# A norm's last multiply as an item of its own, and the routing in eight pieces, among the scan units on VectorE

## The chip, the cores and the metric

The kernel runs on one core of one Trainium2 chip. The metric is the device time of one execution in microseconds (us); less is better. The engines are called TensorE (PE, with PEld for its weight loads), VectorE (DVE), ScalarE (ACT), GpSimd (POOL) and SyncE (SP, which here only issues DMAs).

## What is computed

The input is x of 8 batches x 256 positions x 256 features. Each batch passes three blocks in turn:

```
x = x + 0.5 * ffn(layernorm(x))      # f1
x = x + mamba_block(layernorm(x))    # mixer, then MLP
x = x + 0.5 * ffn(layernorm(x))      # f2, the same weights as f1

ffn(x):     scores = sigmoid(x @ gate_w)           # 32 experts
            top 6 of the scores, divided by their sum -> combine
            sum over experts of combine * (silu(x@wg) * (x@wu)) @ wd,  plus a shared expert
block(x):   h = x + mixer(rmsnorm(x));  h + mlp(rmsnorm(h))
mixer(h):   projections z, x, B, C, dt;  conv of 4 taps;  dt = softplus(...)
            h_t = exp(dt*A) * h_(t-1) + dt*x*B     # 512 channels x 16 states, over 256 positions
            y = sum over states of h_t * C;  y * silu(z) @ out_proj
```

Every expert is computed for every position (26 chunks of 128 hidden features: 24 routed, 2 shared), and the combine weights zero most of them.

## The kernel before, in words

Data lie with features on partitions and positions along the free dimension. The program is a list of **items** for each step t (`items_of`, from L129), and every engine walks the same list and does its own part of each item (`walk`). The steps overlap the batches: in step t batch t is in f1 (`first`), batch t-1 in the mixer (`mamba`), batch t-2 in the MLP (`mlp`) and batch t-3 in f2 (`second`). Steps t=3 to t=6 have everything in them and are four turns of a hardware loop; the others are written out, from t=-1 (load, norm and routing of the first batch) to t=10.

**The heavy list** is the MLP's chunks (`gum`, `down`) and the feed-forward's chunks. Chunk p is made of `g` (6 matmuls in three passes over split halves, L595 to L597), ScalarE's tanh (L824), `by_g` (VectorE, L957), `u` (6 matmuls), `by_u` (VectorE, L963), `by_comb` (GpSimd multiplies by the combine weights, L1218) and `down` (L675). f1 and f2 share the chunks: their positions lie side by side, 512 columns. There are three PSUM banks for `g` and `u` (`gub`) and three for everything small (`side`); an engine that wants a bank waits until the use three before it has been read.

**The light list** is norms and projections (`along`), then 32 scan **units** with the norms and routings among them, then `yz`, `outp` and the norm rms2. A unit is one pair of states of 128 channels: `ub` is a matmul that spreads B (L765) and VectorE's product (L1103), on ScalarE two exponentials (L921); `unit` is VectorE's scan (L1112), a matmul that spreads C (L768), VectorE's product (L1118) and GpSimd's add to a sum (L1228, L1231). After the eighth unit of a group GpSimd adds the halves and the sum to y (L1234, L1238). `yz` (L1122) gates y when the last sum is there.

**A norm** is `n1` and `n2`. For ln1, lnA and ln2 `n1` is a mean on TensorE (L690), VectorE's subtraction (L1001) and ScalarE's square (L834); for rms1 and rms2 only the square. `n2` is the mean of the squares on TensorE (L698), ScalarE's Ln and Exp with -0.5 into the one `rstd` tile (L837, L840, each with its table load), and VectorE's multiply by rstd: L1015 for ln1, ln2 and lnA, two of L1011 for rms1 and rms2. **A routing** `rt1` is 8 small matmuls (L711), ScalarE's exp (L843), and on VectorE `route` (L1131): 19 instructions that count up the semaphore `routing`, most of them waiting for the one before them. `rt2` in the next step uses its result.

**The order** comes from `merge` (L176): two lists are laid over each other by the share of their summed lengths (`LENGTH` where f1 and f2 are both there, else `SHORT`). First the units and the two norm-and-routing chains are merged (ln2's chain in the first half of them, ln1's in the second), and the result, behind `along`, is merged with the heavy list. On VectorE and GpSimd `late_order` then sets an item back by up to `LAG` items, but not past the next light item. `GROWS` tells by how much each item raises each semaphore, and `USES` who frees a `side` bank; the waits are worked out from them.

Of the kernel before, what the change touches and what calls it, by code (L numbers as in the profile page):

```python
# [35 lines left out]
KC = DM // P  # L36
EXPERTS, FEXP, TOPK, FSH = 32, 96, 6, 192
# [8 lines left out]
TT = SEQ // P  # L46
# [9 lines left out]

GROWS = {
# [50 lines left out]
def kind_of(item):  # L108
# [3 lines left out]
    if item[0] == "n2":  # L112
        return "n2r" if item[1] in ("rms1", "rms2") else "n2c"
# [14 lines left out]

def items_of(t):  # L129
# [4 lines left out]
    if t < 0:  # L134
        return [("load",), ("n1", "ln1"), ("n2", "ln1"), ("rt1", "f1")]
# [4 lines left out]
    norms = [("n1", "lnA"), ("n2", "lnA"), ("n1", "rms1"), ("n2", "rms1")] if mamba else []  # L140
# [15 lines left out]
    if not mamba:  # L156
# [11 lines left out]
SHORT = {"n1": 3, "n2": 8.0, "split": 2.25, "x": 5, "z": 3,  # L168
          "dt": 3, "sp": 3, "sp_dt": 3, "sp_x": 2, "y0": 2,
          "ub": 2, "unit": 2, ("unit", UNITS - 1): 8, "rt1": 8,  # L170
# [39 lines left out]
def ffn_items(t, first, second):  # L210
# [8 lines left out]
    for p in range(FFN_CHUNKS + DLAG):  # L219
# [20 lines left out]
LAG = {"n1": 0, "n2": 3, "split": 0, "x": 0, "z": 1, "dt": 0, "sp": 1, "sp_dt": 0,  # L240
       "sp_x": 0, "y0": 0, "ub": 0, "unit": 1, "rt1": 3, "outp": 4,
# [9 lines left out]
def late_order(items):  # L251

    out, held, left = [], None, 0
    for it in items:
# [6 lines left out]
        else:  # L261
# [7 lines left out]
    "side": {"n1c": [("centered", 1)], "n2c": [("logged", 1)],  # L269
             "n2r": [("logged", 1)], "rt1": [("rt_exp", 1)], "rt2": [("comb_ready", 1)],  # L270
# [47 lines left out]
def macaron_kernel(nc, d):  # L318
# [13 lines left out]
    with ctx:  # L332
# [249 lines left out]
        def _(pe):  # L582
# [18 lines left out]
            def do(s, it):  # L601
# [99 lines left out]
                elif kind == "rt1":  # L701
# [3 lines left out]
                    pe.wait_ge(sem["normed"], s.count("normed", ("n2", norm), 1))  # L705
# [20 lines left out]
                elif kind in ("z", "x", "split"):  # L726
                    if kind == "split" and it[1] == 0:
                        pe.wait_ge(sem["normed"], s.count("normed", ("n2", "rms1"), KC))
# [57 lines left out]
        def _(act):  # L786
# [5 lines left out]
            def do(s, it):  # L792
# [33 lines left out]
                elif kind == "n1":  # L826
# [3 lines left out]
                    elif it[1] == "rms1":  # L830
                        act.wait_ge(sem["normed"], s.count("normed", ("n2", "lnA"), 1))
                    else:
                        act.wait_ge(sem["mixed"], s.count("mixed", ("outp",), 1))
# [94 lines left out]
        def _(dve):  # L928
# [13 lines left out]
            def do(s, it):  # L942
# [48 lines left out]
                elif kind == "r0":  # L991

                    dve.wait_ge(sem["normed"], s.count("normed", ("n2", "lnA"), 1))
# [9 lines left out]
                elif kind == "n2":  # L1003
                    dve.wait_ge(sem["rstd"], s.count("rstd", it, 1))
# [11 lines left out]
                elif kind == "rt1":  # L1016
# [114 lines left out]
            def route(s, it):  # L1131


                done = [0]
# [14 lines left out]
                for tt in range(TT):  # L1149
                    link(v.max(top8[:, tt, :], sc[:, tt, 0:EXPERTS]))  # L1150
                settle()
                link(v.tensor_copy(top8[:, :, TOPK:8], marks[:]))
                settle()
                link(v.memset(pace[:], 0.0))
                for tt in range(TT):
                    link(v.match_replace(rep[:, tt, :], top8[:, tt, :], sc[:, tt, :], 0.0))
                settle()
                link(v.tensor_tensor(cm[:], sc[:, :, 0:EXPERTS], rep[:, :, 0:EXPERTS], ALU.subtract))
                settle()
                link(v.tensor_reduce(csum[:], cm[:], axis=AX.X, op=ALU.add))  # L1160
                settle()
                link(v.tensor_scalar(csum[:], csum[:], 1e-20, None, ALU.add))
                settle()
                link(v.reciprocal(csum[:], csum[:]))
                settle()
                for tt in range(TT):
                    link(v.tensor_scalar(cm[:, tt, :], cm[:, tt, :], csum[:, tt:tt + 1], None, ALU.mult))
                settle()
                E = EXPERTS
                out = c3[it[1]]  # L1170
                link(v.tensor_copy(out[:, :, 0:E], cm[:]))
                settle()
                link(v.tensor_tensor(cm[:], cm[:], out[:, :, 0:E], ALU.subtract))
                settle()
                link(v.tensor_copy(out[:, :, E:2 * E], cm[:]))
                settle()
                link(v.tensor_tensor(out[:, :, 2 * E:3 * E], cm[:], out[:, :, E:2 * E], ALU.subtract))
                assert done[0] == 19
# [139 lines left out]
```

## Time and profile before

| | us |
|---|---|
| median of 3 executions | 1938.59 (1936.56 to 1942.36) |
| the profiled execution, its time | 1936.02 |
| its span, first to last instruction | 1934.2 |
| mean granted TensorE clock in it | 0.934 of full speed |

Times within the profile count from the start of the span. The rows of the section below are of this one execution. In them a line number is one of the kernel before; "busy" is the time in which an engine had an instruction, and the idle time before an instruction stands in brackets with what ended it. PEclk is the clock that TensorE was granted, as a share of 2.4 GHz.

### The profile page before, as it was taken

To read this page: it belongs to the slowest core of one execution; us is meant where nothing else is said; L and a number is where in the kernel's file an instruction comes from. 1 tells how busy PE (TensorE), PEld (TensorE's weight loads), DVE (VectorE), ACT (ScalarE), POOL (GpSimd) and SP (SyncE) were. 2 spreads that over 40 slices of the span, in tenths; PEclk is the share of its full clock that TensorE was granted. 3 is DMA by queue.
4 is the path that set the end of the run, shared out by engine and by line. 5 is a ranking of instruction groups with operands and counts; after the bars stand their busy time and mean duration, and the time that the engine had idled before them with its cause. 6 is when DMAs were issued, how large, how long until landed. Compare 5 with 4: busy or idle time off the path is not lost. (4 is left out here: it accounts for less than half of the span.)

```text
span 1934.2 us, 25234 instructions
## 1 busy us (share of the span) xinstructions
PE 1601.1 (83%) x7512; PEld 1194.2 (62%) x7512; DVE 1295.1 (67%) x2331; ACT 705.1 (36%) x1418; POOL 720.2 (37%) x838
## 2 busy tenths in 40 slices
PE   6776768677978988789888989788988998678999
PEld 5665557555755557455664557555675567556888
DVE  3236984688468964789466974689648974896343
ACT  4234424433352425333343423433244334432211
POOL 4411552244134532345223542245324542353222
PEclk9887889878999999899998999899999999988999
DMA  7752223323232222222231223222232223323563
GB/s 260 281 170 91 86 86 99 111 88 98 78 106 72 81 89 74 105 74 80 80 104 65 84 77 95 85 77 88 81 98 93 87 77 86 126 88 101 174 205 133
DMA packets 72751, 204.77 MB, mean 106 GB/s; under 512 B 12928, under 2 KB 22368, under 8 KB 72224
## 3 DMA queue, kind: packets, MB, share of 16 engines
q1 hardware_dynamic: 64416, 177.86, 27.7%
q0 software_dynamic: 8192, 25.17, 4.5%
q8 instruction: 69, 1.13, 0.2%
q14 instruction: 74, 0.61, 0.1%
HBM read 179.39 MB, written 15.73 MB: 101 GB/s over the span
## 5 line engine op out<-in xcount | busy, mean ns | idle before, releaser
L595 PE MATMUL gub<-x_hi,wr 128*128 128x256 f32 (+1 forms) x1144 | 460.5, 403 | 83.5 <-DVE hid L963 60.6
L675 PE MATMUL acc<-hid,w_down 128*128 128x256 f32 (+1 forms) x1144 | 423.9, 498 | 0.9 <-DVE hid L963 0.8
L1218 POOL TENSOR_TENSOR hid<-hid,weight 128x256 f32<-128x256 f32 (+1 forms) x264 | 263.5, 998 | 428.0 <-DVE hid L963 409.9
L824 ACT ACTIVATE hid<-gub 128x256 f32<-128x256 f32 (+1 forms) x350 | 160.9, 460 | 680.5 <-PE gub L597 590.5
L596 PE MATMUL gub<-x_lo,wr 128*128 128x256 f32 (+1 forms) x1144 | 395.7, 346 | 0.0
L597 PE MATMUL gub<-x_hi,wr 128*128 128x256 f32 (+1 forms) x1144 | 394.7, 345 | 0.0
L1231 POOL TENSOR_TENSOR ring<-ring 128x512 f32<-128x512 f32 x192 | 245.8, 1280 | 314.4 <-DVE ring L1118 314.4
L1112 DVE TENSOR_TENSOR_SCAN ring<-decays,side 128x512 f32<-128x512 f32 x256 | 310.7, 1214 | 4.1 <-DVE side L1103 1.5
L595 PEld LDWEIGHTS gub<-x_hi,wr 128*128 128x128 f32 x1144 | 231.9, 203 | 122.1 <-issue 73.9
L675 PEld LDWEIGHTS acc<-hid,w_down 128*128 128x128 f32 x1144 | 212.9, 201 | 88.3 <-issue 68.8
L596 PEld LDWEIGHTS gub<-x_lo,wr 128*128 128x128 f32 x1144 | 232.3, 203 | 21.1 <-issue 4.3
L597 PEld LDWEIGHTS gub<-x_hi,wr 128*128 128x128 f32 x1144 | 230.5, 201 | 23.5
L921 ACT ACTIVATE decays<-dts,a_neg 128x255 f32<-128x255 f32 x512 | 223.5, 497 | 50.8 <-DVE ring L1112 40.8
L957 DVE SCALAR_TENSOR_TENSOR hid<-hid,gub 128x256 f32<-128x256 f32 (+1 forms) x286 | 153.7, 537 | 97.0 <-ACT hid L824 97.0
L1103 DVE TENSOR_TENSOR side<-dtx,side 128x512 f32<-128x512 f32 x256 | 176.8, 690 | 31.2 <-PE side L765 30.7
L1118 DVE TENSOR_TENSOR ring<-ring,side 128x512 f32<-128x512 f32 x256 | 176.0, 688 | 32.1 <-PE side L768 6.5
L963 DVE TENSOR_TENSOR hid<-hid,gub 128x256 f32<-128x256 f32 (+1 forms) x286 | 153.7, 537 | 52.1 <-PE gub L597 49.8
L768 PE MATMUL side<-cst,sel_c 96*128 96x256 bf16 x512 | 108.1, 296 | 80.6 <-DVE ring L1112 76.0
L765 PE MATMUL side<-bst,sel_b 96*128 96x256 bf16 x512 | 108.8, 297 | 50.4 <-DVE ring L1112 40.6
L1197 POOL TENSOR_TENSOR pool_pace<-eps_col 128x1 f32<-128x1 f32 x128 | 29.6, 231 | 297.5 <-PE gub L637 183.0
L768 PEld LDWEIGHTS side<-cst,sel_c 96*128 96x128 bf16 x512 | 37.3, 103 | 148.9 <-DVE ring L1112 102.9
L739 PE MATMUL side<-dts,w_in 128*128 128x256 f32 x448 | 110.3, 395 | 21.4 <-DVE z L1028 12.6
(115 smaller groups left out, 1725.4 us busy)
## 6 DMA issues: line engine op xcount, KB each, us to landing
wr<-w_halves SPq DMA_DIRECT2D x260, 512.0 KB, 3.3
wm_gu<-in_w_mlp POOLq DMA_DIRECT2D x64, 256.0 KB, 3.0
w_halves<-wr SPq DMA_DIRECT2D x26, 512.0 KB, 4.9
wm_down<-in_w_mlp POOLq DMA_DIRECT2D x64, 128.0 KB, 2.6
w_raw<-in_w_gu SPq DMA_DIRECT2D x26, 256.0 KB, 4.7
cst<-decays SPq DMA_DIRECT2D x192, 32.0 KB, 1.9
xin<-in_x SPq DMA_DIRECT2D x8, 256.0 KB, 3.4
x<-in_x SPq DMA_DIRECT2D x8, 256.0 KB, 2.6
```

The source lines that it names most:

```text
L595: mm(out, w[:, 0, half, k, :], x_hi[:, k, a:b], start=(k == 0), stop=False)
L596: mm(out, w[:, 0, half, k, :], x_lo[:, k, a:b], start=False, stop=False)
L597: last = mm(out, w[:, 1, half, k, :], x_hi[:, k, a:b], start=False, stop=(k == KC - 1))
L675: last = mm(acc[k][:, a:b], w, h[:, a:b], start=(c == 0), stop=(c == (MLP_CHUNKS if mlp else FFN_CHUNKS) - 1))
L824: A(hid[c % HSLOTS][:, a:b], s.gub_of(it)[:, a:b], ACT.Tanh, scale=0.5).then_inc(sem["tanh_done"], 1)
L921: A(decay[u % 2][:, h, 1:SEQ], dts[:, j, 1:SEQ], ACT.Exp, scale=a_neg[:, j, n:n + 1]).then_inc(sem["decay"], 1)
L957: v.scalar_tensor_tensor(h, h, 1.0, s.gub_of(of)[:, a:b], ALU.add, ALU.mult).then_inc(sem["gated"], 1)
L1103: v.tensor_tensor(b, twice(dtx[:, j, :]), b, ALU.mult).then_inc(sem["driven"], 1)
L1112: v.tensor_tensor_scan(w.rearrange("p h s -> p (h s)"), decay[u % 2][:, :, :].rearrange("p h s -> p (h s)"), s.side_of(("ub", u))[:, :], 0 ...
L1118: v.tensor_tensor(w, w, pair(s.side_of(it)), ALU.mult).then_inc(sem["read_out"], 1)
L1218: nc.gpsimd.tensor_tensor(h, h, weight[c // 3 % CSLOTS][:, a:b], ALU.mult).then_inc(sem["weighted"], 1)
L1231: add(ysum, ysum, ring[:, u % 3], ALU.add).then_inc(sem["y_sum"], 1)
```

## The change

`n2` ends with rstd on ScalarE; VectorE's multiply is the new item `nm`, placed behind it by the length of `n2` (3, or 6 in `SHORT`). `rt1` ends with ScalarE's exp; VectorE's 19 instructions become eight items `rq` of 2, 3, 1, 3, 2, 2, 2 and 4 instructions, each of length 0.75. The order within a routing and the instructions are as before; each piece but the first begins with a wait for the piece before it. `LAG` is 3 for `nm` and 0 for `n2`, `rt1` and `rq`, so on VectorE a routing is no longer set back. Those who waited for `n2`'s product now wait for `nm`'s. Cut to its core:

```diff
+ROUTE = (2, 3, 1, 3, 2, 2, 2, 4)
...
-    "n2c": {"side_filled": 1, "logged": 1, "rstd": 1, "normed": 1},
-    "n2r": {"side_filled": 1, "logged": 1, "rstd": 1, "normed": KC},
-    "rt1": {"side_filled": 1, "rt_exp": 1, "routing": 19},
+    "n2": {"side_filled": 1, "logged": 1, "rstd": 1},
+    "nmc": {"normed": 1},
+    "nmr": {"normed": KC},
+    "rt1": {"side_filled": 1, "rt_exp": 1},
+    **{f"rq{i}": {"routing": links} for i, links in enumerate(ROUTE)},
...
+def norm(which):
+    return [("n1", which), ("n2", which), ("nm", which)]
+
+
+def routing(call):
+    return [("rt1", call)] + [("rq", call, i) for i in range(len(ROUTE))]
...
-    norms = [("n1", "lnA"), ("n2", "lnA"), ("n1", "rms1"), ("n2", "rms1")] if mamba else []
+    norms = norm("lnA") + norm("rms1") if mamba else []
...
-    last = [("yz",), ("outp",), ("n1", "rms2"), ("n2", "rms2")] if mamba else []
+    last = [("yz",), ("outp",)] + norm("rms2") if mamba else []
...
-    ln2 = [("n1", "ln2"), ("n2", "ln2"), ("rt1", "f2")] if mlp else []
-    ln1 = [("n1", "ln1"), ("n2", "ln1"), ("rt1", "f1")] if following else []
+    ln2 = norm("ln2") + routing("f2") if mlp else []
+    ln1 = norm("ln1") + routing("f1") if following else []
...
-LENGTH = {"n1": 3, "n2": 5, "split": 2.25, "x": 10.0, "z": 3,
+LENGTH = {"n1": 3, "n2": 3, "nm": 2, "rq": 0.75, "split": 2.25, "x": 10.0, "z": 3,
...
-          "ub": 2, "unit": 2, ("unit", UNITS - 1): 8, "rt1": 8,
+          "ub": 2, "unit": 2, ("unit", UNITS - 1): 8, "rt1": 2,
...
-SHORT = {"n1": 3, "n2": 8.0, "split": 2.25, "x": 5, "z": 3,
+SHORT = {"n1": 3, "n2": 6.0, "nm": 2.0, "rq": 0.75, "split": 2.25, "x": 5, "z": 3,
...
-LAG = {"n1": 0, "n2": 3, "split": 0, "x": 0, "z": 1, "dt": 0, "sp": 1, "sp_dt": 0,
-       "sp_x": 0, "y0": 0, "ub": 0, "unit": 1, "rt1": 3, "outp": 4,
+LAG = {"n1": 0, "n2": 0, "nm": 3, "rq": 0, "split": 0, "x": 0, "z": 1, "dt": 0, "sp": 1, "sp_dt": 0,
+       "sp_x": 0, "y0": 0, "ub": 0, "unit": 1, "rt1": 0, "outp": 4,
...
-                elif kind == "n2":
-                    dve.wait_ge(sem["rstd"], s.count("rstd", it, 1))
+                elif kind == "nm":
+                    dve.wait_ge(sem["rstd"], s.count("rstd", ("n2", it[1]), 1))
...
-                dve.wait_ge(sem["rt_exp"], s.count("rt_exp", it, 1))
-                link(v.tensor_scalar(e_sc[:], e_sc[:], 1.0, None, ALU.add))
-                settle()
-                link(v.reciprocal(sc[:, :, 0:EXPERTS], e_sc[:]))
-                settle()
-                link(v.memset(pace[:], 0.0))
...
+                if piece == 0:
+                    dve.wait_ge(sem["rt_exp"], s.count("rt_exp", ("rt1", it[1]), 1))
+                    link(v.tensor_scalar(e_sc[:], e_sc[:], 1.0, None, ALU.add))
+                    settle()
+                    link(v.reciprocal(sc[:, :, 0:E], e_sc[:]))
+                else:
+                    settle()
+                if piece == 1:
+                    link(v.memset(pace[:], 0.0))
+                    for tt in range(TT):
+                        link(v.max(top8[:, tt, :], sc[:, tt, 0:E]))
+                elif piece == 2:
+                    link(v.tensor_copy(top8[:, :, TOPK:8], marks[:]))
+                elif piece == 3:
+                    link(v.memset(pace[:], 0.0))
+                    for tt in range(TT):
+                        link(v.match_replace(rep[:, tt, :], top8[:, tt, :], sc[:, tt, :], 0.0))
+                elif piece == 4:
+                    link(v.tensor_tensor(cm[:], sc[:, :, 0:E], rep[:, :, 0:E], ALU.subtract))
+                    settle()
+                    link(v.tensor_reduce(csum[:], cm[:], axis=AX.X, op=ALU.add))
+                elif piece == 5:
+                    link(v.tensor_scalar(csum[:], csum[:], 1e-20, None, ALU.add))
+                    settle()
+                    link(v.reciprocal(csum[:], csum[:]))
+                elif piece == 6:
+                    for tt in range(TT):
+                        link(v.tensor_scalar(cm[:, tt, :], cm[:, tt, :], csum[:, tt:tt + 1], None, ALU.mult))
+                elif piece == 7:
+                    link(v.tensor_copy(out[:, :, 0:E], cm[:]))
+                    settle()
+                    link(v.tensor_tensor(cm[:], cm[:], out[:, :, 0:E], ALU.subtract))
+                    settle()
+                    link(v.tensor_copy(out[:, :, E:2 * E], cm[:]))
+                    settle()
+                    link(v.tensor_tensor(out[:, :, 2 * E:3 * E], cm[:], out[:, :, E:2 * E], ALU.subtract))
+                assert done[0] == ROUTE[piece]
```

## Rows read from the trace of the kernel before

**Rows 1.** The page: span, and busy time with its share of the span.

```profile
span 1934.2 us, 25234 instructions
PE 1601.1 (83%) x7512; PEld 1194.2 (62%) x7512; DVE 1295.1 (67%) x2331; ACT 705.1 (36%) x1418; POOL 720.2 (37%) x838
```

**Rows 2.** Windows by step, t=3, t=5 and t=7: window, its length, then each engine.

```profile
core 0: us, PE busy (x) PEld busy (x) DVE busy (x) ACT busy (x) POOL busy (x), PEclk, DMA share, GB/s
498.00:717.00 219.00, 187.80 (x775) 126.84 (x773) 159.01 (x272) 84.07 (x161) 84.83 (x92) 0.98 0.26 83
942.00:1167.00 225.00, 194.09 (x780) 131.00 (x780) 158.87 (x271) 84.07 (x161) 85.02 (x92) 0.95 0.26 84
1392.00:1594.00 202.00, 184.41 (x766) 125.32 (x765) 153.38 (x250) 79.76 (x155) 83.80 (x92) 0.98 0.29 91
```

**Rows 3.** Windows of stages within t=5, among the scan units; same columns.

```profile
1012.50:1062.00 49.50, 39.94 (x151) 24.94 (x149) 34.74 (x62) 15.82 (x31) 18.30 (x16) 0.86 0.20 65
1034.00:1052.00 18.00, 16.67 (x75) 10.77 (x73) 15.00 (x33) 5.90 (x13) 10.27 (x9) 1.00 0.19 63
1062.00:1144.30 82.30, 75.05 (x323) 46.63 (x322) 76.20 (x117) 31.35 (x65) 44.06 (x37) 1.00 0.25 84
1028.40:1033.80 5.40, 5.40 (x15) 3.99 (x16) 2.50 (x4) 0.00 (x0) 1.28 (x1) 0.50 0.23 77
1055.80:1061.10 5.30, 5.30 (x12) 2.70 (x13) 1.56 (x3) 0.82 (x2) 0.17 (x1) 0.50 0.00 0
1122.30:1144.00 21.70, 19.07 (x84) 11.99 (x84) 20.86 (x28) 6.47 (x14) 11.62 (x10) 1.00 0.22 74
```

**Rows 4.** Timeline of t=5 at the norms ln2 and ln1: start, us, instruction, idle before.

```profile
1025.85 0.69 DVE L1015 TENSOR_TENSOR xc_f<-xc_f,rstd 128x512 f32<-128x512 f32 x1 [4.10 <-ACT rstd L840]
1028.33 0.61 PE L768 MATMUL side<-cst,sel_c 96*128 96x256 bf16 x2 [4.16 <-DVE ring L1112]
...
1099.39 0.69 DVE L1015 TENSOR_TENSOR xc_f<-xc_f,rstd 128x512 f32<-128x512 f32 x1 [2.38 <-ACT rstd L840]
```

**Rows 5.** Timeline of t=5 at f2's routing, its first and last instruction among them.

```profile
1048.05 0.20 DVE L1144 TENSOR_SCALAR e_sc<-e_sc 128x64 f32<-128x64 f32 x1 [0.94 <-ACT e_sc L843]
...
1049.19 1.03 DVE L1152 COPY top<-marks 128x4 f32<-128x4 f32 x1
...
1052.92 0.23 DVE L1177 TENSOR_TENSOR c_f<-cm,c_f 128x64 bf16<-128x64 f32 x1
...
1055.74 0.61 PE L768 MATMUL side<-cst,sel_c 96*128 96x256 bf16 x2 [3.42 <-DVE ring L1112]
```

**Rows 6.** Groups by line (busy us, mean ns, idle), then single lines (ns min/median/max).

```profile
L1231 POOL TENSOR_TENSOR ring<-ring 128x512 f32<-128x512 f32 x192 | 245.8, 1280 | 314.4 <-DVE ring L1118 314.4
L1112 DVE TENSOR_TENSOR_SCAN ring<-decays,side 128x512 f32<-128x512 f32 x256 | 310.7, 1214 | 4.1 <-DVE side L1103 1.5 <-ACT decays L921 0.8
L1144 DVE TENSOR_SCALAR e_sc<-e_sc 128x64 f32<-128x64 f32 x16 | 8.5, 532 | 7.9 <-ACT e_sc L843 7.9
L1152 DVE COPY top<-marks 128x4 f32<-128x4 f32 x16 | 7.5, 470 | 0.6
...
L1152 DVE COPY top<-marks x16: 169/171/1054, 16.2 to 1840.9; 128x4 f32<-128x4 f32 x16
L1158 DVE TENSOR_TENSOR cm<-sc,rep x16: 224/226/785, 17.4 to 1841.6; 128x64 f32<-128x64 f32 x16
```

**Rows 7.** Waits over the whole span: us in total, times, longest.

```profile
DVE xc_f L1015 <- ACT rstd L840: 50.6, 16, 5.1
DVE xs L1122 <- POOL xs L1238: 19.4, 8, 2.7
```

**Rows 8.** TensorE's first projection behind rms1 in t=5; VectorE's multiply of an MLP chunk.

```profile
962.58 3.72 PE L739 MATMUL side<-dts,w_in 128*128 128x256 f32 x16 [1.09 <-DVE dts L1011]
...
L949 DVE TENSOR_TENSOR hid<-hid,gub 128x256 f32<-128x256 f32 x64 | 26.9, 421 | 2.2
```

More of the change, by code:

```diff
@@ L111, in kind_of @@
         return "n1r" if item[1] in ("rms1", "rms2") else "n1c"
-    if item[0] == "n2":
-        return "n2r" if item[1] in ("rms1", "rms2") else "n2c"
+    if item[0] == "nm":
+        return "nmr" if item[1] in ("rms1", "rms2") else "nmc"
+    if item[0] == "rq":
+        return f"rq{item[2]}"
     if item[0] in ("wl", "wln"):
@@ L134, in items_of @@
     if t < 0:
-        return [("load",), ("n1", "ln1"), ("n2", "ln1"), ("rt1", "f1")]
+        return [("load",)] + norm("ln1") + routing("f1")
     hand = ([("hx", "f1")] if first else []) + ([("hx", "f2")] if second else [])
@@ L159, in items_of @@
     return hand + heavy[:6] + keep + merge(heavy[6:-TAIL], along + scan, length) + heavy[-TAIL:]
-LENGTH = {"n1": 3, "n2": 5, "split": 2.25, "x": 10.0, "z": 3,
+LENGTH = {"n1": 3, "n2": 3, "nm": 2, "rq": 0.75, "split": 2.25, "x": 10.0, "z": 3,
           "dt": 3, "sp": 3, "sp_dt": 3, "sp_x": 2, "y0": 2,
-          "ub": 2, "unit": 2, ("unit", UNITS - 1): 8, "rt1": 8,
+          "ub": 2, "unit": 2, ("unit", UNITS - 1): 8, "rt1": 2,
           "yz": 3.9, "outp": 3, "g": 1.3, "u": 1.3, "down": 1.7, "gum": 1.7, "cmb": 0.2}
-SHORT = {"n1": 3, "n2": 8.0, "split": 2.25, "x": 5, "z": 3,
+SHORT = {"n1": 3, "n2": 6.0, "nm": 2.0, "rq": 0.75, "split": 2.25, "x": 5, "z": 3,
           "dt": 3, "sp": 3, "sp_dt": 3, "sp_x": 2, "y0": 2,
-          "ub": 2, "unit": 2, ("unit", UNITS - 1): 8, "rt1": 8,
+          "ub": 2, "unit": 2, ("unit", UNITS - 1): 8, "rt1": 2,
           "yz": 3.9, "outp": 3, "g": 1.3, "u": 1.3, "down": 1.7, "gum": 1.7, "cmb": 0.2}
@@ L268 @@
 USES = {
-    "side": {"n1c": [("centered", 1)], "n2c": [("logged", 1)],
-             "n2r": [("logged", 1)], "rt1": [("rt_exp", 1)], "rt2": [("comb_ready", 1)],
+    "side": {"n1c": [("centered", 1)], "n2": [("logged", 1)],
+             "rt1": [("rt_exp", 1)], "rt2": [("comb_ready", 1)],
              "z": [("z_done", 1)], "x": [("x_padded", 1)],
@@ L704, in do @@
                     norm = "ln1" if it[1] == "f1" else "ln2"
-                    pe.wait_ge(sem["normed"], s.count("normed", ("n2", norm), 1))
+                    pe.wait_ge(sem["normed"], s.count("normed", ("nm", norm), 1))
                     for over, least in s.last_use("side", it):
@@ L727, in do @@
                     if kind == "split" and it[1] == 0:
-                        pe.wait_ge(sem["normed"], s.count("normed", ("n2", "rms1"), KC))
+                        pe.wait_ge(sem["normed"], s.count("normed", ("nm", "rms1"), KC))
                         if first_mamba[0]:
@@ L830, in do @@
                     elif it[1] == "rms1":
-                        act.wait_ge(sem["normed"], s.count("normed", ("n2", "lnA"), 1))
+                        act.wait_ge(sem["normed"], s.count("normed", ("nm", "lnA"), 1))
                     else:
@@ L991, in do @@
                 elif kind == "r0":
-                    dve.wait_ge(sem["normed"], s.count("normed", ("n2", "lnA"), 1))
+                    dve.wait_ge(sem["normed"], s.count("normed", ("nm", "lnA"), 1))
                     if ("end", "mlp") in s.at:
@@ L1015, in do @@
                         v.tensor_tensor(dst[:], dst[:], twice(rstd[:, :]), ALU.mult).then_inc(sem["normed"], 1)
-                elif kind == "rt1":
+                elif kind == "rq":
                     route(s, it)
@@ L1131, in route @@
             def route(s, it):
+                E = EXPERTS
+                out, piece = c3[it[1]], it[2]
                 done = [0]
@@ L1141, in settle @@
                     dve.wait_ge(sem["routing"], s.count("routing", it, done[0]))
-                dve.wait_ge(sem["rt_exp"], s.count("rt_exp", it, 1))
-                link(v.tensor_scalar(e_sc[:], e_sc[:], 1.0, None, ALU.add))
-                settle()
-                link(v.reciprocal(sc[:, :, 0:EXPERTS], e_sc[:]))
-                settle()
-                link(v.memset(pace[:], 0.0))
-                for tt in range(TT):
-                    link(v.max(top8[:, tt, :], sc[:, tt, 0:EXPERTS]))
@@ L1151, in route @@
[L1151 to L1178, printed above, removed]
+                if piece == 0:
[5 more added lines that the diff above has]
+                    settle()
```

## The prediction

> **What bounds the kernel now.** The page's busy times come first [rows 1]: TensorE is busy 83% of the span, VectorE 67%. Neither share says what a change on VectorE is worth, because the work differs by stage. The windows by step [rows 2] show that the steps with everything in them take 219 to 225 us, of which TensorE is busy 188 to 194 and VectorE 159. Step numbers are those of the planner; t=3 to t=6 are four turns of one loop. The stages of one such turn [rows 3] show more. From 1062 to 1144.3, among the scan units, VectorE is busy 76.20 of 82.30 us, and in a quiet piece of it 20.86 of 21.70, so 0.96 is what it reaches: VectorE sets the pace there. From 1012.5 to 1062 it is busy only 34.74 of 49.50 us, and TensorE 39.94, although the same mix of work stands there. So something is waited for.
>
> The chain of waits in order of time says what. At 1025.85 VectorE begins a norm's last multiply after 4.10 us of idling for ScalarE's rstd [rows 4]. The chunk's gating and the scan are queued behind that multiply, so 2.5 us later TensorE has itself been idle for 4.16 us. The second pair of events is the routing: it runs from 1048.05 to 1053.15 in one piece, and TensorE then restarts after 3.42 us [rows 5]. TensorE comes out of both gaps with a granted clock of 0.50, that is 1.2 instead of 2.4 GHz: it is busy 5.40 and 5.30 us at that level [rows 3], which loses half of them. The step's other norm waits 2.38 us on VectorE [rows 4], and its routing lies in the stage that VectorE bounds anyway.
>
> **The change, part by part.** Lengths add up as before (5 = 3 + 2, 8 = 6 + 2, and 8 = 2 + 8 x 0.75), so every other item keeps its place; what moves is VectorE's part of norms and routings.
>
> *The multiply among the units.* ln2's "nm" stands 3/32 of the units' 134 lengths behind "n2", 12.6 lengths or about three units. The wait that it replaces is 4.10 us [rows 4]. Between the two places VectorE now has three units, each a scan of 1.21 us [rows 6] and two multiplies of 0.69 such as stand at 1099.39 [rows 4], so 3 x 2.6 = 7.8 us, and two chunks' gating. That covers the wait, and it goes to nothing; without the cover the 4.10 would be back. Who needs the product is "rt1" on TensorE, 2/32 later (four unit items), with a buffer rotation of three between them: no new wait.
>
> *The routing.* Its instructions stay 19 links. Eight pieces come about every 3.1 lengths, three quarters of a unit and its "ub" (4 lengths). Inside the burst some 0.5 us goes between dependent links, and seven new borders let a neighbour overlap: I take 0.8 us less for each routing, bounds 0 and 1.2; its 5.1 us otherwise stay VectorE's. The first wait of a piece is on a link long done: nothing. The last two pieces of ln1's routing stand at 127.7 and 130.9 of 134, behind the last unit's start at 126, so they fall into the wait of the gate "yz" for GpSimd, 19.4 us in eight [rows 7], 2.4 each; they carry 1.5 us out of the full stage.
>
> *GpSimd's adds.* Now the price. A copy of 4 columns takes 169 ns at the least and 1054 at the most, a small subtraction 224 and 785 [rows 6]; the long one at 1049.19 [rows 5] stands while GpSimd works. The Trainium skill, "SBUF — State Buffer", section "Who interferes with whom", says that copies, casts, scalings and operations with two SBUF inputs need ports that GpSimd uses too, and that the later of two waits until the first has finished. GpSimd's adds last 1.28 us [rows 6] and it is busy 44.06 of 82.30 us in the full stage [rows 3]. In the burst mostly the first copies pay, since GpSimd soon runs out of work: the sum behind the exponential costs 532 in the mean against some 200 where it stands free, at 1048.05 [rows 5], the copy 470 against 169, so 0.64 us a routing [rows 6]. Spread, six pieces begin with such an instruction. At that mean of 0.32 each they pay 1.9, with 0.4 for those further inside a piece 2.3 us: 1.6 more than now. Lower bound 0 more; upper bound ten such links of a routing, all held 0.86 (1.03 less 0.17): 8.6, or 7.9 more. I take 1.6, nearest to the mean rows. By the skill's rule alone ten links would each find GpSimd at work with the share 0.54 and wait half an add, 3.4 us; that would be 1.2 us more a routing than my figure, 18 us over fifteen routings, and the median 1913. Net of the overlap a routing costs 0.8 us more.
>
> *rms1 and rms2.* In the mixing block rms1's multiply was ahead of MLP chunk 5's two multiplies on VectorE and is now behind them. TensorE waits for it at "split": today 1.09 us [rows 8]. The two multiplies take 0.42 us each [rows 8], 0.84 together, and the tanh before them may come later than rstd: 1.0 us more in each full step, bounds 0 and 2. lnA's multiply keeps its place on VectorE. rms2's goes behind the last chunk's gating, with 5 us of down projections covering it: nothing.
>
> **The sum.** One full step, first stage (49.5 us): TensorE needs 39.94 less half of 10.70, 34.6 at the full clock; at its best share there, 16.67 of 18.00, that is 37.3 us. VectorE needs 34.74 + 0.8 at 0.96: 37.0. So at most 12.2 us can go. At least 4.2 should, the norm's gap alone. Two engines that are both nearly full with three buffers between them don't reach both limits; I take 7. Second stage: 2.4 (the wait) + 1.5 (two pieces) - 0.8 (routing) - 0.3 (the multiply may meet an add): 2.8. rms1: -1.0. Together 8.8, times four turns 35.2 us.
>
> The other steps: 16 waits of such multiplies sum to 50.6 us [rows 7]; four turns hold 4 x 6.48 = 25.9, eight waits the other 24.7, 3.1 each. The two in the first steps, at most 5.1 each by the row's longest, I count at nothing: the first stays where it was, the second stands in t=0, where the weights still arrive. Six give 18.5, less seven routings at 0.8, 5.6: 12.9. Where VectorE isn't full this doesn't all reach the end, as at t=7 with 153 of 202 us [rows 2]; two thirds, 8.6. Sum 43.8 us. The profiled execution took 1936.0 us (1.8 around its span), 2.6 below the median of 1938.6: 1892.2 there, 1895 as a median.
>
> **Rivals.** (a) *VectorE is the bound in both stages*, and TensorE's gap after the routing is only its lead, used up: then just the multiplies' waits go, 50.6 less 10.2 at the start, and 15 spread routings lose 1.6 each to GpSimd. 40.4 - 24 is 16, 1922; with some of the clock back 1915. For it: the 0.96 from 1122 to 1144; against it: the clock row of 0.50 and the unequal halves. (b) *Both limits are reached*: 12.2 instead of 7, four times, 1874. For it: both engines' needs come out alike. (c) *Slower: GpSimd's adds.* A piece behind a scan unit meets the add which that unit's product has just released. If seven of ten such links are held 0.86 us, a routing pays 6.0 instead of 0.64, 5.4 more and with the overlap 4.6. Against my 0.8 that is 3.8 x 15 = 57 us: 1952. It decides from 2.9 us a routing above my 0.8 (43.8 / 15): held time of 0.64 + 0.8 + 3.7 = 5.1 us, six held links of ten. Against it: a small link starts at once behind the product, ahead of the add. This is the skill's rule of the held second engine, made the worst of. (d) *The wait only moves*: TensorE stalls as long at rt1 or at the gating behind the pieces: no change. Against it: all consumers stand four items or more behind.
>
> **How the numbers follow.** Forecast 0.50, (a) 0.24, (b) 0.13, (c) 0.07, (d) 0.06. A measurement of this kernel tells about 0.3%, 6 us, from no change. Faster by more: forecast, (b) and nearly all of (a), 0.86; within 0.06; slower 0.08. The range holds the forecast, (a), and (b) to its edge: 1872 to 1924.
>
> **What would show it.** In the changed profile: the idle time before the norm's multiply in xc_f near 0 instead of 50.6 us; no 4 us gap of TensorE at the c selection after it; in the stage that now runs from 1012.5 to 1062 a granted clock near 1.00 instead of 0.86; turns of about 216 us; TensorE's idle time before "split" up to 2 us; the 4-column copy with a mean of 0.5 to 0.8 us instead of 0.47, and the sum of VectorE up by 10 to 25 us. I am wrong if turns stay above 221 us with the waits gone (then (a)), or if the small links' mean passes 0.6 us all over (then (c)).

## The result, and the profile after

The changed kernel takes 1908.01 us in the median of 4 executions (1904.27 to 1911.02), beside 1938.11 for the kernel before on the same chip: a ratio of 0.9835, with an interval of 0.9813 to 0.9857. It is faster by 30 us; the forecast was 43.8 in the sum and 1895 as a median, with a range of 1872 to 1924. The profiled execution took 1911.02 us.

The page of the changed kernel, its span and busy times, answers to [rows 1]:

```profile
span 1909.2 us, 25234 instructions
PE 1600.1 (84%) x7512; PEld 1197.6 (63%) x7512; DVE 1318.9 (69%) x2331; ACT 703.8 (37%) x1418; POOL 724.8 (38%) x838
```

VectorE is busy 23.8 us more with the same instructions. TensorE's busy time is what it was (1600.1 after 1601.1) for the same matmuls; a better clock would have lowered it. That is the first sign that half clock has gone in one place and come in another.

The waits, over the whole span, answer to [rows 7]:

```profile
DVE xc_f L1030 <- ACT rstd L855: 5.1, 1, 5.1
PE side L754 <- DVE dts L1026: 16.6, 8, 2.3
PE side L783 <- DVE ring L1127: 38.9, 54, 2.3
PE side L664 <- DVE ring L1127: 39.7, 28, 3.6
```

and in the kernel before, TensorE's waits at the selection of c and at the spreading of the combine weights:

```profile
PE side L768 <- DVE ring L1112: 76.0, 67, 4.2
PE side L649 <- DVE ring L1112: 23.3, 21, 1.7
```

Of the 50.6 us in which VectorE waited for rstd, 5.1 are left, the one wait before the first step. The wait of y's gate for GpSimd is off the list. TensorE's longest wait at the selection of c (L783) is 2.3 us; it was 4.16 [rows 4] and 3.42 [rows 5]. But TensorE's wait for rms1 ahead of the first projection (L754) is longer: 16.6 us in eight. And a part of the waiting has moved: the waits at the selection of c fell from 76.0 to 38.9 us, while those at the matmul that spreads the combine weights (L664, L649 before) rose from 23.3 to 39.7, the longest from 1.7 to 3.6.

Windows of the changed kernel: t=5 from its start to the end of the MLP item, t=5 from there to its end, the four full turns together, the stage in which ln2's norm and f2's routing begin, and 3.4 us of the projection behind the wait for rms1. Columns as in [rows 2].

```profile
929.40:974.60 45.20, 40.21 (x173) 33.09 (x173) 22.39 (x54) 16.22 (x30) 12.56 (x32) 0.96 0.31 90
974.60:1147.80 173.20, 151.91 (x608) 97.11 (x607) 139.81 (x218) 67.51 (x132) 73.13 (x60) 0.96 0.26 85
493.80:1366.30 872.50, 767.56 (x3125) 521.33 (x3123) 649.20 (x1082) 335.02 (x644) 342.69 (x368) 0.96 0.27 86
1003.10:1052.00 48.90, 44.70 (x191) 28.55 (x190) 43.96 (x67) 19.66 (x40) 24.69 (x21) 0.97 0.26 87
952.80:956.20 3.40, 3.40 (x10) 2.69 (x9) 0.66 (x2) 1.07 (x3) 0.00 (x0) 0.51 0.00 0
```

The same three stretches of work in the kernel before, and its projection behind rms1:

```profile
941.20:984.00 42.80, 38.22 (x173) 32.03 (x173) 22.39 (x55) 16.26 (x30) 12.31 (x32) 1.00 0.33 96
984.00:1166.50 182.50, 155.87 (x607) 98.97 (x607) 136.78 (x219) 67.81 (x132) 72.71 (x60) 0.93 0.24 81
497.40:1391.80 894.40, 770.33 (x3124) 520.41 (x3122) 636.28 (x1083) 336.29 (x644) 340.24 (x368) 0.96 0.26 84
962.60:966.00 3.40, 3.40 (x16) 3.02 (x17) 1.02 (x3) 0.67 (x3) 0.00 (x0) 1.00 0.00 0
```

The second part of t=5, projections and scan units, went from 182.5 to 173.2 us: 9.3 gained. The first part, where MLP and mixing block's norms run, went from 42.8 to 45.2: 2.4 lost. (The first part's windows do not begin at the same instruction: 1.9 us ahead of the turn's first MLP matmul before, 1.1 us ahead of it now. The windows below do.) The last line of each block is 3.4 us of the same projection: sixteen matmuls at a clock of 1.00 before, ten at 0.51 now. Before, that window begins with the projection; now it begins 1.25 us behind the projection's start, where the clock falls. Four turns gave 21.9 us, all other steps together 25.0 - 21.9 = 3.1: the first full turn begins 3.6 us earlier, and what follows the last one takes 0.5 more.

Windows of t=5 that begin and end at the same instructions in both kernels show more: from the turn's first MLP matmul to its first scan, from there to the tenth scan, and from there to the last. Before:

```profile
943.10:1012.00 68.90, 58.59 (x245) 46.53 (x246) 38.77 (x79) 31.35 (x58) 17.40 (x36) 0.95 0.33 103
1012.00:1061.40 49.40, 39.84 (x151) 24.97 (x150) 34.64 (x62) 16.20 (x32) 18.80 (x16) 0.86 0.20 65
1061.40:1141.70 80.30, 73.05 (x315) 45.02 (x313) 74.33 (x116) 31.35 (x65) 43.31 (x36) 1.00 0.26 86
```

The changed kernel:

```profile
930.50:1002.70 72.20, 60.69 (x245) 47.68 (x246) 39.13 (x82) 31.40 (x58) 17.68 (x36) 0.93 0.32 98
1002.70:1035.70 33.00, 30.79 (x138) 19.86 (x138) 28.72 (x39) 14.65 (x29) 17.50 (x15) 1.00 0.25 81
1035.70:1122.90 87.20, 77.86 (x326) 48.10 (x325) 80.36 (x132) 32.51 (x68) 45.29 (x37) 0.98 0.25 85
```

3.3 us are lost ahead of the first scan, 16.4 are gained up to the tenth, and 6.9 are lost behind it. The last two belong together. Before, f2's routing stood in one block behind the eighth scan [rows 5]. Now its first piece comes behind the tenth,

```profile
1038.86 0.37 DVE L1162 TENSOR_SCALAR e_sc<-e_sc 128x64 f32<-128x64 f32 x1
```

and its last ends at 1064.78, behind the sixteenth. So all of this routing has left the stretch in which VectorE was busy 34.64 of 49.40 us, and has gone into the one in which it was busy 74.33 of 80.30.

Why the stretch ahead of the first scan is longer, tells the timeline of the changed kernel in t=5 around rms1:

```profile
948.75 0.42 ACT L855 ACTIVATE rstd<-rstd 128x256 f32<-128x256 f32 x1
...
949.75 0.42 DVE L962 SCALAR_TENSOR_TENSOR hid<-hid,gub 128x256 f32<-128x256 f32 x1 [3.20 <-ACT hid L839]
950.21 0.42 DVE L964 TENSOR_TENSOR hid<-hid,gub 128x256 f32<-128x256 f32 x1
950.54 0.88 DVE L1026 SCALAR_TENSOR_TENSOR dts<-hn,lnw,rstd 128x256 f32<-128x256 f32 x2
...
951.55 5.40 PE L754 MATMUL side<-dts,w_in 128*128 128x256 f32 x16 [2.33 <-DVE dts L1026]
```

rstd is there at 949.17. VectorE is in front of the MLP chunk's multiply, waits for its tanh until 949.75, does its two multiplies, and only then rms1's. TensorE waits 2.33 us instead of 1.09 [rows 8], and the 16 matmuls behind it take 5.40 us instead of 3.72.

The routing's small instructions, groups by line of the changed kernel (busy us, mean ns, idle before), answer to [rows 6]:

```profile
L1249 POOL TENSOR_TENSOR ring<-ring 128x512 f32<-128x512 f32 x192 | 246.7, 1285 | 318.6 <-DVE ring L1133 318.6
...
L1187 DVE TENSOR_SCALAR cm<-cm,csum 128x32 f32<-128x32 f32 x32 | 18.7, 626 | 0.1
L1193 DVE CAST c_f<-cm 128x64 bf16<-128x64 f32 x16 | 12.9, 803 | 0.6
L1162 DVE TENSOR_SCALAR e_sc<-e_sc 128x64 f32<-128x64 f32 x16 | 8.0, 498 | 2.3 <-ACT e_sc L858 2.3
L1172 DVE COPY top<-marks 128x4 f32<-128x4 f32 x16 | 4.4, 276 | 0.0
```

Not the copy pays, as the forecast had it, but the products (L1187) and the cast (L1193). How such a hold looks, in the timeline of the changed kernel:

```profile
1057.90 1.27 POOL L1249 TENSOR_TENSOR ring<-ring 128x512 f32<-128x512 f32 x1 [2.48 <-DVE ring L1133]
...
1058.85 1.61 DVE L1187 TENSOR_SCALAR cm<-cm,csum 128x32 f32<-128x32 f32 x2
1059.13 1.30 POOL L1236 TENSOR_TENSOR hid<-hid,weight 128x512 f32<-128x512 f32 x1
1060.38 1.20 DVE L1127 TENSOR_TENSOR_SCAN ring<-decays,side 128x512 f32<-128x512 f32 x1
```

Two products that last 0.23 us each where nothing stands against them take 1.61: they end with GpSimd's second instruction (1060.43), which began right behind the first. All 19 links of a routing sum to 4.74 us in the mean before, to 7.11 after, and to 4.0 in the last one, where GpSimd has nothing to do: held time has gone from 0.7 to 3.1 us a routing.

### The profile page after: what moved, and what is told of

It is laid out like the page before. It is cut to its first block and busy times, and to the rows that moved or that the text cites. A ratio compares the mean times of both kernels' runs of the same rounds, so it can differ in the third digit from the quotient of the medians.

```text
span 1909.2 us, 25234 instructions
## 1 busy us (share of the span) xinstructions
PE 1600.1 (84%) x7512; PEld 1197.6 (63%) x7512; DVE 1318.9 (69%) x2331; ACT 703.8 (37%) x1418; POOL 724.8 (38%) x838
## 5 line engine op out<-in xcount | busy, mean ns | idle before, releaser
L690 PE MATMUL acc<-hid,w_down 128*128 128x256 f32 (+1 forms) x1144 | 419.4, 494 | 0.8 <-DVE hid L978 0.8
L1236 POOL TENSOR_TENSOR hid<-hid,weight 128x256 f32<-128x256 f32 (+1 forms) x264 | 266.6, 1010 | 384.0 <-DVE hid L978 366.6
L783 PE MATMUL side<-cst,sel_c 96*128 96x256 bf16 x512 | 106.2, 291 | 42.8 <-DVE ring L1127 38.9
L754 PE MATMUL side<-dts,w_in 128*128 128x256 f32 x448 | 115.8, 410 | 28.4 <-DVE dts L1026 16.6
L652 PE MATMUL gub<-xn_mlp,wm_gu 128*128 128x256 f32 x512 | 120.4, 384 | 0.5 <-issue 0.2
```

Of the source, the lines that this page charges most:

```text
L690: last = mm(acc[k][:, a:b], w, h[:, a:b], start=(c == 0), stop=(c == (MLP_CHUNKS if mlp else FFN_CHUNKS) - 1))
L1236: nc.gpsimd.tensor_tensor(h, h, weight[c // 3 % CSLOTS][:, a:b], ALU.mult).then_inc(sem["weighted"], 1)
```

## The experiments

All twelve kernels start from the changed one. Each result is the median and the ratio to the kernel before on the same chip, with its interval. The kernels ran on three chips, so where two results lie close, the ratios are the better comparison. "Turns" is the time of t=3 to t=6 in the profiled execution, read with the window query as above: 894.4 us before, 872.5 after. It is one execution of each kernel, while the executions of one kernel lie up to 12 us apart, so a difference of two or three us in the turns shows little.

**Where the missing 14 us are.** e1 puts rstd and the multiply of the mixing block's norms back together; ln1, ln2 and the routings stay spread.

```diff
-LENGTH = {"n1": 3, "n2": 3, "nm": 2,
+LENGTH = {("n2", "lnA"): 0, ("nm", "lnA"): 5, ("n2", "rms1"): 0, ("nm", "rms1"): 5,
+          ("n2", "rms2"): 0, ("nm", "rms2"): 5, "n1": 3, "n2": 3, "nm": 2,
```

(`SHORT` likewise, with 0 and 8.) e4 does it for rms1 alone.

> The changed kernel with the multiplies of lnA, rms1 and rms2 put back right behind their n2 (so on VectorE where they were before the change); ln1, ln2 and the pieces stay. Theory A: rms1's multiply behind the MLP chunk's gating is what lengthens the MLP and projection stage, from 42.8 to 45.1 us in a full turn and by 19 us over seven steps, half of it TensorE's longer wait and half its fallen clock. Then this stage is back at 42.8 us, the scan stage stays at 173.2, and the time is about 1889 us (ratio 0.975 to before). Rival B: the scan stage takes in whatever the MLP stage gives, since VectorE bounds it: 1905 us or more.

> The changed kernel with rms1's multiply alone put back. Theory A: rms1 is all of the loss in the MLP stage, so the same as the kernel with all three put back within 3 us, about 1889 to 1892 us. Rival: lnA or rms2 carries some of it, 1895 to 1905 us.

e1: 1887.68 us, 0.9729 [0.9703, 0.9754]; e4: 1891.66, 0.975 [0.9727, 0.9773]. e1 came out as theory A had it (it said 1889), and beats both kernels: 20 us faster than the change, 50 faster than before. e4 is at the upper end of its theory A; rms1 is some 16 of the 20. In e1's timeline TensorE waits as it did before the change:

```profile
940.39 0.42 ACT L855 ACTIVATE rstd<-rstd 128x256 f32<-128x256 f32 x1
940.94 0.88 DVE L1026 SCALAR_TENSOR_TENSOR dts<-hn,lnw,rstd 128x256 f32<-128x256 f32 x2 [2.74 <-ACT rstd L855]
...
941.95 3.72 PE L754 MATMUL side<-dts,w_in 128*128 128x256 f32 x16 [1.09 <-DVE dts L1026]
```

Here VectorE waits 2.74 us for rstd, and that is right: TensorE is the one that needs the product. Windows of e1, both parts of t=5 and the four turns:

```profile
920.50:963.40 42.90, 38.27 (x174) 32.02 (x173) 22.32 (x54) 16.11 (x30) 12.38 (x32) 1.00 0.31 95
963.40:1134.50 171.10, 149.56 (x607) 95.78 (x607) 140.74 (x218) 67.73 (x132) 73.18 (x60) 0.98 0.25 86
492.60:1350.40 857.80, 754.35 (x3123) 513.15 (x3122) 649.73 (x1082) 335.16 (x644) 342.34 (x368) 0.98 0.27 87
```

The first part is back at 42.9. Against the change the four turns are 14.7 us shorter: 13.2 of it is busy time of TensorE (767.56 to 754.35), the same matmuls at a better clock, and only 1.5 idle time. 14.2 of the 14.7 lie ahead of the first scan (table below). VectorE waits 42.7 us for rstd at rms1's and rms2's multiplies in e1 and 5.2 in the change, and e1 is the faster kernel all the same.

**The two halves of the change.** e2 has all five norms together as before and only the routing in pieces. e3 has the routing whole, with the lengths 0 for `rt1` and 8 for `rq` and a `LAG` of 3, and only ln1's and ln2's multiplies apart:

```diff
-    return [("rt1", call)] + [("rq", call, i) for i in range(len(ROUTE))]
+    return [("rt1", call), ("rq", call)]
```

> All multiplies right behind their n2, the routing in eight pieces: the pieces alone. Theory A: the gap of 3.4 us after f2's routing and its half clock go, 5 to 6 us in a full turn, less 2.5 us held time in each of two routings: 1 to 2 us less in a turn, 1930 to 1938 us in all, as before within 0.4%. Rival: the pieces carry the gain, 1915 us or less. Other rival: the held links decide, 1945 us or more.

> The multiplies of ln1 and ln2 apart, all other norms as before, the routing in one piece with its lag of 3: the norm's part alone. Theory A: the waits of 4.1 and 2.4 us go with the clock loss of the first, 7 to 8 us in a full turn, and the gap after the routing stays: 1900 to 1910 us. Rival B (VectorE is the bound, the gap of TensorE is only its lead): 1915 to 1922 us.

e2: 1925.54, 0.9935 [0.9912, 0.9958], 12.6 us gained; turns 885.4. This is better than theory A's 1930 to 1938 and far from the 1915 of the first rival, so none of the three expectations was met. e3: 1900.95, 0.9812 [0.9787, 0.9836], 37.1 gained; turns 866.9; within theory A's bounds. 12.6 + 37.1 is 49.7, and e1, which has both, gained 50.4: the halves add up. Three quarters of e1's gain is the multiply of ln1 and ln2. In a full turn it is worth (894.4 - 866.9) / 4 = 6.9 us and the pieces (894.4 - 885.4) / 4 = 2.3, together 9.1 before rounding. The two stretches of e3's t=5, first to tenth and tenth to last scan, show where: 8.6 us shorter than before up to the tenth scan, 0.3 behind it.

```profile
999.60:1040.40 40.80, 35.17 (x153) 22.59 (x152) 34.75 (x63) 16.16 (x32) 18.79 (x16) 1.00 0.24 78
1040.40:1120.40 80.00, 72.28 (x313) 44.52 (x311) 74.51 (x115) 31.35 (x65) 43.69 (x36) 1.00 0.26 86
```

**What the held instructions cost.** e5 is e1 with GpSimd's adds of the scan on one column (all four kinds of them, one is shown), e6 the same in e3. Both leave the sum over the states out of the output.

```diff
-add(ysum, ysum, ring[:, u % 3], ALU.add)
+add(ysum[:, :, 0:1], ysum[:, :, 0:1], ring[:, u % 3, :, 0:1], ALU.add)
```

> The mixer's multiplies near, ln1 and ln2 apart, eight pieces, and GpSimd's adds of the scan cut to one column each (so the sum over the states is left out of the output): what holds the routing's small links is gone but for the multiply by the combine weights. Theory P (the held links are GpSimd's adds): a routing's links sum to at most 5.0 us instead of 7.2, near the 4.02 that they take where nothing holds them. To be compared with the next kernel, whose routing is whole. Theory P1 (held time is paid at the end): the pieces are worth 13 us + some 25 us against the whole routing. Rival P2 (VectorE has slack where they stand): still 13 us.

> The same with the routing whole and its lag of 3, GpSimd's adds again of one column. The routing's links sum to about 4.2 us instead of 4.7. Time under P1 35 to 40 us above the kernel with pieces, under P2 13 us above it.

e5: 1854.57, 0.9562 [0.9544, 0.9581]; e6: 1874.79, 0.9656 [0.9637, 0.9676]. The difference is 20 us, where the full adds leave 13: between the two theories. The windows of the four turns, of e5 and then of e6, tell more:

```profile
477.30:1322.40 845.10, 760.13 (x3125) 516.12 (x3123) 627.72 (x1082) 334.91 (x644) 205.21 (x368) 0.97 0.27 89
```

```profile
495.10:1340.00 844.90, 748.79 (x3125) 507.45 (x3122) 633.72 (x1082) 336.31 (x644) 205.04 (x368) 0.99 0.28 88
```

In the full turns the two are equal; the difference lies in the other steps, most of it (495.1 - 477.3 = 17.8 us) ahead of the first full turn. What makes it there was not looked for. TensorE is busy 11.3 us more in e5's turns than in e6's, and the turns last the same. The test was less clean than meant: a routing's links still sum to 5.07 us in e5 and to 4.48 in e6, where at most 5.0 and about 4.2 were expected; GpSimd's multiply of the hidden chunk (L1236), left whole, can still hold them. The one thing it shows is that taking most of the adds away does not make the pieces worth more in a full turn; they are then worth nothing there.

**The number of pieces.** e7 has two pieces (9 and 10 links, each of length 3), e8 four (5, 4, 4 and 6, each of length 1.5), both with e1's norms. e8's grouping:

```diff
+GROUPS = ((0, 1), (2, 3), (4, 5), (6, 7))
```

> The mixer's multiplies near, ln1 and ln2 apart, the routing in two pieces of 9 and 10 instructions. Theory P: a burst makes GpSimd run out of work, so only its first holdable links pay, about 0.8 us twice instead of 3.1 a routing, 1.5 us less in 15 routings; two blocks of 2.5 us are still short enough for three buffers. If held time is paid (P1) 1875 to 1884 us. Under P2 and if blocks of 2.5 us stall TensorE: 1888 to 1898 us.

> As the last with four pieces of 5, 4, 4 and 6 instructions. Under P1 between the kernels with two and eight pieces, 1880 to 1888 us; under P2 the same as eight pieces within 3 us, 1885 to 1891 us.

e7: 1891.44, 0.9764 [0.9738, 0.979]; e8: 1906.35, 0.983 [0.9812, 0.9847]. e7 lies within P2's bounds: two pieces are as good as eight within the intervals. Four are worse than both, which neither theory had. Held time is not the reason: the links sum to 5.50 us in e7, 6.64 in e8 and 7.20 in e1. Windows of the four turns, e7 and e8:

```profile
494.40:1352.70 858.30, 749.62 (x3126) 508.90 (x3124) 643.72 (x1082) 335.97 (x644) 341.40 (x368) 0.98 0.27 87
```

```profile
492.20:1359.80 867.60, 760.15 (x3122) 515.81 (x3122) 650.60 (x1083) 335.56 (x644) 342.94 (x368) 0.97 0.27 86
```

e8 is 9.3 us longer there than e7, with 10.5 more of TensorE's busy time and 1.2 less of idle: the half clock again. The timeline of e8 at f2's routing in t=5, and a window behind it:

```profile
1051.93 1.30 POOL L1251 TENSOR_TENSOR ring<-ring 128x512 f32<-128x512 f32 x1 [2.27 <-DVE ring L1136]
...
1052.88 1.61 DVE L1189 TENSOR_SCALAR cm<-cm,csum 128x32 f32<-128x32 f32 x2
...
1055.98 1.21 DVE L1130 TENSOR_TENSOR_SCAN ring<-decays,side 128x512 f32<-128x512 f32 x1
...
1057.25 0.61 PE L784 MATMUL side<-cst,sel_c 96*128 96x256 bf16 x2 [3.42 <-DVE ring L1130]
```

```profile
1056.20:1062.80 6.60, 5.55 (x14) 4.03 (x15) 4.84 (x7) 0.60 (x1) 2.73 (x3) 0.50 0.02 6
```

The last piece, six links with both products held, stands in front of a scan, and TensorE runs dry for 3.42 us at the selection of c, as long as before the change, and comes back at half clock. e1's longest wait there is 2.4. Two further kernels test this: e9 is e8 with the small adds, e10 is e8 with the 19 links divided 2, 7, 6 and 4 (its expectation names the middle two the wrong way round).

> The norms of the mixing block as in e1, the routing in four pieces as in e8, and GpSimd's adds of the scan reduced to one column of each state's positions, as in e5 (the sum over the states is left out of the output by that). e8 was 17 us slower than the eight pieces although its routings' instructions lasted 6.64 us in the mean against 7.20. Theory H: e8 loses because links are held behind GpSimd's adds in a cluster (the routing's four products and copies in front of a scan unit), so that TensorE stands still for 3.42 us and comes out at half clock; with small adds nothing is held, and four pieces stand level with e5: 1848 to 1862, ratio 0.953 to 0.960. Theory L: a piece of four or five links is too long for TensorE's lead at its place, held or not, so the 15 us remain: 1866 to 1876, ratio 0.962 to 0.967.

> As e8, four pieces at the same places with the same lengths, full adds, but the links divided otherwise: 2, 6, 7 and 4 links instead of 5, 4, 4 and 6. If the number of pieces and their places decide, it stays at e8's time, 1900 to 1912, ratio 0.979 to 0.986. If it is a matter of which link happens to meet which add, as theory H has it, it moves by more than 5 us from e8; most likely towards e1 and e7, 1885 to 1898, ratio 0.972 to 0.979, since the last piece, whose cluster goes before TensorE's long gap in e8, is two links shorter.

e9: 1867.73, 0.9616 [0.9591, 0.9641]; e10: 1917.13, 0.9869 [0.9848, 0.9891]. e9's median lies within theory L's 1866 to 1876, but its ratio is just below L's 0.962 and its interval reaches into H's 0.953 to 0.960. By the ratios e9 is some 10 us over e5, and with full adds e8 is some 20 over e1, each with about 6 us either way. So a good part of the loss stays with the adds gone, and how much of it is H's isn't decided, the less as e9's links still sum to 5.63 us. e10 moved by 11 us from e8 (8 by the ratios) with the same number of pieces at the same places, outside the bounds for number and places, but to the slow side, against my guess; its links sum to 7.63 us, 1.0 more than e8's, and TensorE is busy 767.66 us in the four turns, 7.5 more than in e8, of 8.0 in all. So it counts which links stand together. In three pairs, the change and e1, e8 and e7, e10 and e8, the time of the turns follows TensorE's busy time; in e5 and e6 it does not, nor in e7 and e1 (4.7 us less busy in e7, and no shorter). Which rule would give a good division in advance stays open.

**Which routing's pieces.** e11 has f1's routing in eight pieces and f2's whole (all 19 links in one item, `LAG` 3), e12 the opposite; norms as in e1.

```diff
+    if call == "f2":
+        return [("rt1", call), ("rw", call)]
```

> The mixing block's norms near as in e1, f1's routing in eight pieces, f2's routing whole and set back by up to three items, as before the change. In the four full turns e3 (both whole) took 866.9 us and e1 (both in pieces) 857.8, so the pieces are worth 2.3 us a turn. Theory Y: that is VectorE's wait of 2.4 us for GpSimd at the gate of y, which f1's last pieces fill; TensorE's gap of 3.4 us behind f2's whole routing costs nothing. Then the four turns take 856 to 860 us here, the wait stays away, and the median is 1884 to 1893, ratio 0.971 to 0.976. Theory G: the gain is the gap behind f2's routing, so the four turns take 865 to 869 here, the median 1894 to 1902, ratio 0.977 to 0.981.

> The opposite of e11: f2's routing in eight pieces, f1's routing whole. Theory Y: VectorE's wait of 2.4 us at the gate of y is back in every turn, the four turns take 865 to 869 us and the median is 1894 to 1902, ratio 0.977 to 0.981. Theory G: 856 to 860 us in the four turns and 1884 to 1893, ratio 0.971 to 0.976, wait or no wait. e7, whose two pieces left that wait in place and which took 858.3 us in its four turns, speaks for G.

e11: 1894.29, 0.9759 [0.9742, 0.9776]; turns 858.3. e12: 1898.92, 0.9775 [0.9762, 0.9788]; turns 861.0. e11's turns and ratio are theory Y's, though TensorE's longest wait at the selection of c is 3.4 us there again; its median is 1 us above Y's bounds, and the execution with these turns was its fastest (1887.91). e12's median and ratio are Y's, its turns lie between the two theories: with VectorE's wait for GpSimd back (14.9 us in six, nothing in e1), they are 3 us over e1's, not 9, and e7 has that wait too (19.5 us in eight) and no longer turns than e1. So in the turns each routing's pieces alone bring most of the 9.1 us by which e3 and e1 differ (8.6 and 5.9). In the whole time, by the ratios, they bring 10 and 7 us of 16, which add up within the intervals. No single wait carries them.

**Where in a turn the kernels differ.** Sums over t=3 to t=6 in us, from the starts of the instructions in the timelines: the turn's first MLP matmul, its first, tenth and last scan, and the next turn's first MLP matmul.

| | to 1st scan | 1st to 10th | 10th to last | to next turn |
|---|---|---|---|---|
| before | 274.8 | 195.2 | 321.0 | 103.3 |
| the change | 288.0 | 132.2 | 348.6 | 103.5 |
| e1, mixing block's norms near | 273.8 | 132.6 | 348.4 | 103.0 |
| e2, pieces only | 274.1 | 157.3 | 348.5 | 105.4 |
| e3, ln1 and ln2 only | 274.6 | 168.9 | 320.3 | 103.1 |
| e7, two pieces | 274.4 | 132.7 | 352.9 | 98.2 |
| e8, four pieces | 275.0 | 132.5 | 356.1 | 103.8 |
| e10, four pieces otherwise | 276.1 | 132.6 | 367.8 | 98.9 |
| e11, f2's routing whole | 274.9 | 165.1 | 315.0 | 103.3 |
| e12, f1's routing whole | 274.3 | 132.4 | 353.9 | 100.2 |

The multiply of ln1 and ln2 (before to e3) brings 26.3 us up to the tenth scan and 0.7 behind it. f2's pieces mostly move time: from e11 to e1 32.5 us go up to the tenth scan and 33.4 come behind it, so in these executions, with f1's routing in pieces, TensorE's gap behind f2's whole routing cost nothing at the end. From e3 to e12, with f1's routing whole, 36.5 go and 33.6 come. e1, e7, e8 and e10 are alike up to the tenth scan; where the links are grouped matters only behind it.

## Why the prediction was right, and where its terms were off

The direction and the range held, and the norm's part of the mechanism; the sum was 43.8 us against 25.0 between the two profiled executions and 30 between the medians. The median of 1908 lies nearer to the 1915 that rival (a) allows than to the forecast's 1895, so the time alone doesn't tell them apart.

**The scan stage's sum came out, its two terms did not.** Forecast 7 + 2.8 = 9.8 us in a full turn; the scan stage gave 9.3 in t=5, and 9.1 from the halves in e2 and e3. But by the table the first term was 15.8 us a turn (195.2 to 132.2 in four) and not 7, beyond the 12.2 that were to be the most, and the second was a loss of 6.9 (321.0 to 348.6) and not a gain of 2.8. The forecast left f2's routing in the first stage ("VectorE needs 34.74 + 0.8"), while all its pieces came behind the tenth scan. That the two errors nearly cancel is luck. The norm's part of the first term was right: VectorE's wait for rstd is gone, no other took its place at rt1, and e3, which has the norms alone, gains 6.6 us a turn there, above the lower bound of 4.2. The 2.4 us counted in the second stage for ln1's wait gave 0.2 a turn in e3. TensorE's two gaps went below 2.4 us. The clock in the stage at the norm went from 0.86 [rows 3] to 0.97, not quite to the 1.00 forecast.

**The term that was mis-sized to the end is rms1's.** It was 1.0 us in each full step, bounds 0 and 2, priced as VectorE's delay of 0.84 and counted in four turns only. The delay came as written (TensorE's wait grew by 1.24), but ahead of the first scan, where it stands, it took 3.3 us a turn: in t=5 1.24 of waiting and 5.40 - 3.72 = 1.68 for the projection, part of it at half clock, which I had priced for the gaps that go and not for the gap that grows. The remaining 0.4 was not traced. And the mixing block's norms stand in t=1 to t=8, not in four steps. Put back together (e1) they give 14.7 us in the four turns and 20.3 in all, against 4.0 in the sum; rms1 alone (e4) some 16. I also held that lnA and rms2 cost nothing: e1 and e4 differ by 4 us, within reach of their intervals.

**The other steps** were to give 8.6 us and gave 3.1. With the mixing block's norms put back they give 48.3 - 36.6 = 11.7, so the two-thirds rule was on the low side and the miss is again that of the mixing block's norms. Without that term the sum would have been 47.8, and e1 measured 50.4 (48.3 between the profiled executions); as in the scan stage, a sum that fits doesn't make its terms right.

**GpSimd's hold was under-sized, and its cost over-sized.** Forecast 1.6 us more a routing, measured 2.4 (0.7 to 3.1), and on other links: the copy's mean was to rise to between 0.5 and 0.8 us and fell to 0.28, while the products stand at 0.63 and the cast at 0.80. The Trainium skill's rule ("SBUF — State Buffer", "Who interferes with whom"), that the later of the two engines waits until the first has finished, agrees with the trace of the two products above (the second ends at 1060.46, GpSimd's instruction at 1060.43). The prediction's estimate by this rule, 3.4 us held in a routing, was nearer to the measured 3.1 than my 2.3. But the time did not follow the held time: e7 and e1 have the same turns (858.3 and 857.8) with 5.50 and 7.20 us of links, and e2 and e3 together gave 49.7 of e1's 50.4 us, held links and all.

**The rivals.** (a), VectorE as the bound of both stages, 1922 or 1915, falls for the first stage: it shrank by 16.4 us in t=5, and VectorE is busy only 28.72 of its 33.00 us. Its other half, that TensorE's gap after the routing costs nothing, is borne out by e11 for f2's routing. (b), both limits reached, 1874, wasn't met by the change nor by e1. (c), slower, needed 5.1 us held for each routing; it was 3.1, and e10, the worst division, has 3.6 and is still faster than before. (d), the wait moves, is true in part: for rms1, where the consumer stands right behind, and for TensorE's waits at the combine weights, 16.4 us longer in all, while those at the selection of c are 37.1 shorter.

**The signs**: idle before the multiply 5.1 us, as said; no gap of 4 us; turns of 218.1 in the mean, between the 216 forecast and the 221 that would have refuted it; TensorE's wait before the split 2.33 where I had said up to 2; VectorE's sum up by 23.8, within 10 to 25.

## What to carry to other kernels

Setting an instruction apart from its wait pays where its consumer stands far behind it, and costs where another engine waits for the product next: here the same edit gained 37 us at ln1 and ln2 and lost 20 at the mixing block's norms. Look at each place on its own, and price a gap of TensorE that grows as one prices a gap that goes, with the half clock behind it. When two orders of the same instructions differ by about one per cent, compare TensorE's busy time: it shows the clock, though not every difference in it reaches the end (e5 and e6). And when instructions are cut into pieces, look which stretch the pieces come to stand in: here they left one with room on VectorE for one nearly full, and what the first gained the second partly lost again.

## What was not expected of the hardware

A wait of 2.33 us ahead of the projection, after smaller ones, was followed by 3.4 us at 0.51 of the clock, and one of 1.09 us at the same place by none. Yet in e3 TensorE's wait of 3.40 us at the selection of c in t=5 was followed by full clock:

```profile
1036.50:1043.00 6.50, 6.20 (x29) 3.93 (x30) 4.66 (x8) 1.44 (x4) 1.00 (x2) 1.00 0.18 62
```

So the length of one gap doesn't tell whether the clock falls. And the division of each routing's 19 small instructions, without any change in their number, moved this kernel between 1888 and 1917 us (ratios 0.973 to 0.987).
